# Graph network on one core: 6400-byte packets for counts and weights, an earlier load of the K network's inputs, and other groups for two fetches

## The reference, cut to what matters

```python
def get_H(xx):
    z = xx @ W_fc.T
    e = sigmoid(concat([z[src], z[dst]], -1) @ W_attn.T)
    w = exp(e - segment_max(e, dst)[dst])
    h = segment_sum(w / segment_sum(w, dst)[dst] * z[src], dst)
    h1 = segment_sum((h @ W_encK.T + b_encK)[src], dst)
    K = _mlp3(h1, ...)
    ue = (h @ W_p1.T + b_p1)[src] + (h @ W_p2.T + b_p2)[dst]
    U = _mlp3(ue, ...)
    return sum(segment_sum(K[src] * U, dst))
dHdx = grad(get_H)(x)
out = dHdx @ J.T - dHdx @ D.T
```

## Time and profile before

| what | us |
|---|---|
| median of 3 runs | 9009.03 (9007.35 to 9010.03) |
| the profiled execution | 9000.0 |
| its span | 8998.2 |
| busy PE / PEld | 4832.1 / 2528.6 |
| busy DVE / ACT / POOL | 4433.3 / 2687.3 / 5309.9 |

### The profile page before, as it was taken

One profiled execution on the slowest core, in us unless ns is written; L12 is line 12 of the kernel. 1 busy time (PEld: TensorE's weight loads), 2 busy tenths in 40 slices (PEclk: granted clock), 3 DMA queues, 4 the chain that ended last, 5 costly groups with the idle time before them and its releaser, 6 DMA issues.

```text
span 8998.2 us, 77283 instructions
## 1 busy us (share of the span) xinstructions
PE 4832.1 (54%) x27580; PEld 2528.6 (28%) x27580; DVE 4433.3 (49%) x6256; ACT 2687.3 (30%) x2176; POOL 5309.9 (59%) x5420
## 2 busy tenths in 40 slices
PE   1000006999456777775567775545553003519976
PEld 0000005888412222221212222234442002303333
DVE  6789755777300000000089891068886662057760
ACT  0111110000000000000089890046666770047740
POOL 5777777777777777777770005777777756720000
PEclk6555555555577999997689895567776556859976
DMA  9877215444299999999799999755545995859877
GB/s 231 310 292 243 56 52 116 156 149 150 100 414 409 414 410 415 407 411 415 315 271 282 270 284 258 275 176 192 192 178 202 373 368 189 312 154 358 318 259 289
DMA packets 1249731, 2399.37 MB, mean 267 GB/s; under 512 B 567336, under 2 KB 882858, under 8 KB 1227930
## 3 DMA queue, kind: packets, MB, share of 16 engines
q1 hardware_dynamic: 1046906, 2154.96, 67.4%
q0 software_dynamic: 183808, 141.33, 6.4%
q10 hardware_dynamic: 18720, 99.26, 2.9%
HBM read 1616.83 MB, written 696.35 MB: 257 GB/s over the span
## 4 chain that ended last, share of the span: by engine, by line
DMA 32%; POOL 24%; PE 17%; DVE 9%; issue 9%; ACT 4%; DVEq 3%; ACTq 2%; SPq 1%; POOLq 0%
DMA arena<-cells_w 15%; POOL arena L497 11%; POOL cells_w L500 9%; DMA arena<-cells_c 9%; PE ps L756 5%; PE ps L1131 4%; DMA weighed_cells<-arena 4%; POOL xd L500 3%; PE ps L2572 2%; ACT arena L1108 2%; ACTq L1107 2%; DVE ps L2052 1%; PE ps L2565 1%; DMA arena<-hot 1%; ACT arena L1106 1%
## 5 line engine op out<-in xcount | busy, mean ns | idle before, releaser
L756 PE MATMUL ps<-arena 128*64 128x458 f32 (+2 forms) x7252 | 1328.6, 645 | 639.2 <-DMA arena<-cells_w 636.1
L497 POOL DMA_INDIRECT arena<-t_a,arena x832 | 788.5, 948 | 970.0 <-DMA t_a<-arena 716.9
L1131 PE MATMUL ps<-arena 128*33 128x400 f32 x6336 | 1161.9, 522 | 351.9 <-DVE arena L1126 272.9
L500 POOL DMA_INDIRECT sorted<-arena x832 | 883.4, 1062 | 292.9 <-issue 292.9
L500 POOL DMA_INDIRECT cells_c<-arena x832 | 811.7, 976 | 295.6 <-issue 295.6
L497 POOL DMA_INDIRECT arena<-t_kv,idx x832 | 826.9, 994 | 258.8 <-issue 253.2
L500 POOL DMA_INDIRECT cells_w<-arena x832 | 815.0, 980 | 276.8 <-issue 276.8
L500 POOL DMA_INDIRECT xd<-arena x832 | 817.2, 982 | 255.4 <-issue 253.2
L783 DVE COPY carry<-ps 64x128 f32<-64x128 f32 (+1 forms) x5 | 1.5, 295 | 1824.2 <-PE ps L756 1824.2
L756 PEld LDWEIGHTS ps<-arena 128*64 128x64 f32 (+1 forms) x7252 | 429.4, 145 | 1519.8 <-issue 852.4
L1131 PEld LDWEIGHTS ps<-arena 128*33 128x33 f32 x6336 | 368.4, 115 | 1143.2 <-issue 670.5
(11 more groups left out here) (552 smaller groups left out, 9410.8 us busy)
## 6 DMA issues: line engine op xcount, KB each, us to landing
arena<-cells_w SPq DMA_DIRECT2D x245, 3200.0 KB, 25.9
arena<-cells_c SPq DMA_DIRECT2D x294, 800.0 KB, 7.0
arena<-cells_turned SPq DMA_DIRECT2D x200, 800.0 KB, 6.9
cells_w<-arena SPq DMA_DIRECT2D x49, 3200.0 KB
weighed_cells<-arena SPq DMA_DIRECT2D x92, 1600.0 KB, 13.3
arena<-weighed_cells SPq DMA_DIRECT2D x92, 1600.0 KB, 9.8
cells_c<-arena SPq DMA_DIRECT2D x50, 1600.0 KB
cells_turned<-arena SPq DMA_DIRECT2D x100, 800.0 KB, 5.2
```

The lines of the kernel that those rows point to most:

```text
L497: return pool.indirect_dma_start(dst, None, table, bass.IndirectOffsetOnAxis(ap=index, axis=0))
L500: return pool.indirect_dma_start(table, bass.IndirectOffsetOnAxis(ap=index, axis=0), source, None)
L756: mm = pe.matmul(bank[base + k][g * f:(g + 1) * f, 0:m], rows_of, tile[:, g * width + at:g * width + at + m], start=first, stop=last, skip ...
L1131: last = pe.matmul(bank[4 * h + c][64 * kind:64 * kind + 33, 0:400], own[:, t, :], moving[:, 400 * c:400 * c + 400], start=t == 0, stop=do ...
```

## The change

Three things are changed. The limit `max_dma_last_dim` goes from 1600 to 6400 in four DMA statements: the loads of counts in the weighing ahead, the stores of weighed pieces, the loads of the backward attention's ring, and the loads of counts in the attention pass. In SP's order the wait for `hd_made` and the load of SPILLED move behind the broadcasts of `count_s` and the loads of K0 and K1. `HD_AT` goes from 34 to 37 and `GK_AT` from 42 to 41.

```diff
--- before.py
+++ after.py
@@ -379,7 +379,7 @@
         FILLS = 9
         UG = CJ // 8
         CELLS_AT, ENDS_AT = 20, 32
-        ALIAS_AT, XK_AT, GK_AT, HD_AT = 704, 17, 42, 34
+        ALIAS_AT, XK_AT, GK_AT, HD_AT = 704, 17, 41, 37
         GROUPS = J // GROUP
 
         PRODUCTS = [("kvq", 32, 384), ("Wo", 32, 128), ("A", 32, 512), ("D_T", 32, 128), ("L3", 64, 64)]
@@ -1214,14 +1214,14 @@
                 _, _, phase, t, _ = todo[2 * j]
                 p, n = HALVES["ahead"][j]
                 sp.wait_ge(S[f"part_done{p}"], n)
-                sp.dma_start(PART[p], TURNED[t * P:(t + 1) * P, phase * HALF:(phase + 1) * HALF], max_dma_last_dim=1600).then_inc(S[f"part{p}"], 16)
+                sp.dma_start(PART[p], TURNED[t * P:(t + 1) * P, phase * HALF:(phase + 1) * HALF], max_dma_last_dim=6400).then_inc(S[f"part{p}"], 16)
 
             load(0)
             load(1)
             load(2)
             for i, j, _, _, h in todo:
                 sp.wait_ge(S["weighed"], base + 2 * i + 2)
-                sp.dma_start(WEIGHED[i * P:(i + 1) * P, :], AHEAD[i % 3], max_dma_last_dim=1600).then_inc(S[f"weights_kept{i % 3}"], 16)
+                sp.dma_start(WEIGHED[i * P:(i + 1) * P, :], AHEAD[i % 3], max_dma_last_dim=6400).then_inc(S[f"weights_kept{i % 3}"], 16)
                 if h == 1 and 2 * (j + 3) < len(todo):
                     load(j + 3)
 
@@ -1262,7 +1262,7 @@
                 else:
                     source = TURNED[t * P:(t + 1) * P, phase * HALF:(phase + 1) * HALF]
                 to = RING[p] if t in BEFORE else RING[p][:, 0:QUARTER].bitcast(F16)
-                sp.dma_start(to, source, max_dma_last_dim=1600).then_inc(came(p), 16)
+                sp.dma_start(to, source, max_dma_last_dim=6400).then_inc(came(p), 16)
 
         def halves_sp(sp):
 
@@ -1273,7 +1273,7 @@
                 phase, t = PHASES["attend"][k // NS], k % NS
                 if n:
                     sp.wait_ge(S[f"part_done{b}"], n)
-                sp.dma_start(PART[b], tile_rows("c", t)[:, 0, phase * HALF:(phase + 1) * HALF], max_dma_last_dim=1600).then_inc(S[f"part{b}"], 16)
+                sp.dma_start(PART[b], tile_rows("c", t)[:, 0, phase * HALF:(phase + 1) * HALF], max_dma_last_dim=6400).then_inc(S[f"part{b}"], 16)
                 if k == NS + 2:
                     edges_sp(sp)
                 if k == NS + 8:
@@ -2849,13 +2849,13 @@
             sp.wait_ge(S["rows_kept"], 16 * 5)
             others("a_src", AHEAD_OTHER)
             ahead_sp(sp)
-            await_made(sp, "hd_made")
-            sp.dma_start(SPILLED, SPILL).then_inc(S["spilled"], 16)
             for b in range(2):
                 sp.wait_ge(S[f"d_kept{b}"], CREDIT + 16 * IT)
             broadcast(COUNT64S, "count_s", 2, "rows_read")
             for name, to in (("k0", K0), ("k1", K1)):
                 sp.dma_start(to, KEEP[name]).then_inc(S["rows_read"], 16)
+            await_made(sp, "hd_made")
+            sp.dma_start(SPILLED, SPILL).then_inc(S["spilled"], 16)
             sp.wait_ge(S["fm_taken"], STEP["dK"])
             await_made(sp, "gk_made")
             sp.dma_start(by_node(TB["gk"]), nodes(GK, 32)).then_inc(S["tables_kept"], 16)
```

## The result

The changed kernel takes 8952.17 us (median of 4 runs, 8942.35 to 8957.86) against 9009.53 of the kernel before on the same chip (4 runs, 9007.35 to 9013.65): a ratio of 0.9933, interval 0.9921 to 0.9945. That is −57 us in the medians, where −97 was forecast.

The account below looks back on a forecast made before the run. POOL, held by the join behind the weighing ahead's stores, was taken to set the end; −63 − 33 + 3 − 1 − 3 = −97 us, from 9009 to 8912 us, range of 8 in 10 8893 to 8946.

Parts of the forecast that it names:

- What bounds the kernel: Stores hold the weighing ahead; POOL waits 103.26 us for the join behind it, and POOL's last scatter sets the end.
- Sums at group 37: Three groups of POOL's scatters, 21.01 us each, move into its wait for the join: −63.0 us.
- Packets in the weighing ahead: 6400 B packets shorten the stores from 528 to 487 us; the join is written 33.2 us earlier, limited by POOL.
- The inputs beside the join: K network's inputs, loaded earlier, lie beside POOL's join and first fetches and delay them: +3 us, bounds 0 and 8.
- Second chain: PE and DVE's gk and quarter sums run beside POOL, last quarter at 7769; POOL still sets the end by 15 us.
- Attention: Fewer packets for the attention pass's loads of counts, but ACT sets the pace: −1 us, up to 14 possible.
- Backward ring: First loads of the backward attention arrive 8% faster over its first 40 us: −3 us, bounds 0 and −12.
- From the last scatter on: From POOL's last scatter to the kernel's end, the same 1118 us as before, less 3.
- (a): Rival: stores in the weighing ahead do not gain from long packets, join stays at 7450.42; 8944 us, chance 0.15.
- (c): Rival: POOL's small writes queue behind 6400 B packets, +0.53 us each, +208 us; 9120 us, chance 0.05.
- (d): Rival: attention and backward attention gain too, 10 to 20 us more; 8895 us, chance 0.06.
- (e): Rival: the packets do not change because the limit acts differently than its name says; 8946 us, chance 0.02.

Follow-up runs that it names:

- e7: Kernel before with the sums by source fetched after group 20 instead of 34; one execution, 9269.95 us.
- e2: Changed kernel with 1600-byte packets at the four places, so the moves alone; 8955.13 us, 0.9941 against the kernel before.
- e5: Kernel before with each store of a weighed piece replaced by an equal load in 1600 B packets; one execution, 8958.8 us against 9004.73.
- e6: Kernel before with weighed-piece stores replaced by equal loads in 6400 B packets, counts' loads too; one execution, 8949.74 us against 9004.73.
- e1: Kernel before with 6400-byte packets at all four places and nothing moved; 9008.24 us against 9012.41, ratio 0.9997.
- e8: Changed kernel with SP waiting for the written join before loading the K network's inputs; 8946.74 us, 0.9939 against the kernel before.
- e3: Kernel before with only the fetch of the sums by source moved from group 34 to 37; 8964.69 us, 0.9949.
- e4: Changed kernel with the K network's inputs loaded behind the sums again; 8964.13 us, 0.9949 against the kernel before.
- e9: Kernel before with 6400-byte packets only for the loads of counts in the attention pass; 9020.25 us against 9012.04, ratio 1.0004.

## Why the prediction was wrong, step by step

- **What bounds the kernel**: right. The weighing ahead was and is held by its stores, POOL by the join, and POOL sets the end of the stretch (DVE waits 15.49 us for edges, while the quarters are ready).
- **Sums at group 37, −63.0**: right in its place. POOL reached the fetch at 7415.73 (7409.2 forecast; the passes ahead were some 5 us longer in this execution) and had three groups less to do behind the join. What it costs was left out, a term put at nothing without a reason: a group beside the stores lengthens the weighing by 1.9 to 2.3 us (e7, e2), 6.9 us for three (e2).
- **Packets in the weighing ahead, −33.2**: this step failed. It was priced by the ratio of two load rates (380 and 412 GB/s). That ratio was right for loads (395 and 417 in the stage itself, e5 and e6), but this stage stores, and keeps 366 to 371 GB/s at either packet size. Measured: +1 to +3 us in the stage, and 0.9997 for the whole edit (e1). The term is zero or a small loss. POOL's wait for the join was to fall under 12 us and is 47.22. Why stores do not gain stays open. The Trainium skill (DMA: Bandwidth & Descriptors, Specifications), by which 1600 B already gives line rate, would have had this term at zero, as the stores showed (371 and 366 GB/s), and is 5.6% off for the loads. The prediction let the load rates outvote it, without a row of a store.
- **The inputs beside the join, +3 (0 to 8)**: +6.4 for the write, within the bounds (e8 takes it away). The estimate used the write's quiet landing; a row with loads beside it would have been nearer.
- **Second chain 15 us ahead**: confirmed as an order of events, with less room: the last quarter 7.8 us ahead of the last scatter in after. The inputs' wait and PE's stop for alias rows are gone, as forecast. With the inputs left where they were, the quarters come 5.1 and 5.7 us behind POOL (e3, e4), against 6 forecast; what the move is worth in time stays open (e4).
- **Attention, −1**: no gain, perhaps a loss of some 5 us (e9). **Backward ring, −3**: from the store of t_b to the end, seven kernels with 1600 B in the ring took 922.2 to 928.9 us (mean 924.5) and nine with 6400 B 917.1 to 922.5 (mean 919.8); −4.7. This is the one place where the packets seem to pay, and these are loads; the ring was not changed alone in an otherwise equal kernel, and the two ranges touch (922.2 and 922.5), so the 4.7 us rest on the traces.
- **From the last scatter on, 1118 less 3**: 1119.8 in after. The unchanged part grew by 5 us. SP issues the first loads of the ring right behind the last quarter (7828.64), and they now lie beside the landing of the last scatter (5.89 us) and the first load of the pass (4.25 us). In the kernel before, that load took 3.57 us and the scatter's landing less than half:

```profile
7879.98 2.52 DMA xd<-arena
```

So 10.2 us pass from the scatter to DVE instead of 6.1. The other executions fit: 5.8 to 7.6 us where the last quarter comes 13 to 17 us ahead of the last scatter, 8.9 where it comes 10.5 us ahead (e7). This was not foreseen; it is the price of both chains ending together. No run moved these loads alone at an equal lead, so the cause rests on this order.
- **Rivals**: (a), stores that do not gain, is what happened; its 8944 needs +7 for the groups, and then gives 8951. That this falls within 1 us of 8952.17 is partly luck: it lacks the packets' loss, the join's write and the late start of the pass (+2, +6, +5), of which the ring gives back only a few us. It had 0.15. (c), POOL's small writes behind long packets: not as priced, the scatters' mean is 982 ns on POOL in the page of after, as in that of before:

```profile
L500 POOL DMA_INDIRECT xd<-arena x832 | 817.2, 982 | 255.5 <-issue 253.4
```

POOL's transfers do land later beside long packets: its loads of edges took 6.6 us to land before, and 8.3 and 8.9 in after and e1 (7000 to 7300 us). POOL did not wait for them, so this cost nothing. (d) did not show, (e) fell with the count of packets. The sum as it should have been: −63 for the groups, +7 for their cost beside the stores, +2 for the packets there, +6 at the join, +5 behind the last scatter, −5 in the ring, together −48. The two profiles show −42, or −47.5 without the later start of the weighing ahead; the medians show −57. The 9 us between −48 and −57 are explained by no row; executions of one kernel lie some 15 us apart.

## What to carry to other kernels

Price a DMA term with a row of the same direction and mix: a ratio measured on loads says nothing of a stage that stores. Work moved into a wait isn't free when the transfers that end that wait share its engines, so multiply it by what a unit of it costs beside them. When a transfer is brought forward, ask which short transfers it will lie beside: 4.9 MB beside a join cost 6 to 8 us at both joins tried here.

## What was not expected of the hardware

- Loads and stores answer differently to packet length: loads 395 to 417 GB/s from 1600 to 6400 B; the mix with four fifths stores 371 and 366 GB/s.
- With 6400 B packets the queue's share fell to 89.9% at an unchanged rate. The rate by slices of the same stretch is also less even (306 to 405 GB/s, against 354 to 379 with 1600 B).
- A scatter takes POOL 980 to 983 ns with packets of either length, but a group of them slows the stores: from 7060 to 7300 us a piece took 5.98 us beside POOL's scatters (before) and 5.41 us while POOL waited (e7), though POOL's queue carries only 7.7 of 111 MB (before, 7000 to 7300 us).
- The join's write, which landed in 2.2 us in a quiet stretch, took 8.6 us beside 4.9 MB of loads; POOL stood idle 1.50 and 7.91 us behind it.
